# A graph kernel's edge stage in 16-bit halves, with the basis laid out four times and read by blocks of 16 lanes

## The reference

```python
p1 = tanh(h @ pp_W1 + pp_b1) @ pp_W2 + pp_b2
inter = concat(p1[src], p1[dst]) @ pi_W1 + pi_b1
inter = (inter @ pi_W2 + pi_b2) @ pi_W3
i1 = einsum('ecb,eb->ec', inter.reshape(E, 64, 8), edge_attr_8)
i1 = tanh(i1 @ ii_W1 + ii_b1) @ ii_W2 + ii_b2
x = x + segment_sum(i1, dst)
```

## Time and profile before

| | |
|---|---|
| median of 3 runs | 8050.49 us (8045.1 to 8051.35) |
| the profiled execution | 8058.17 us, of which the span is 8056.5 |
| PE, matmuls | 7250.3 us busy (90% of the span), 44520 instructions |
| PE, weight loads | 4945.0 us (61%) |
| DVE | 3022.3 us (38%) |
| ACT | 2022.9 us (25%) |
| POOL | 1563.6 us (19%) |
| DMA queue of SP (q1) | 1816.94 MB, 74.5% of the 16 DMA engines' span |

### The profile page before, as it was taken

One profiled execution on the slowest core, in us unless ns is written; L12 is line 12 of the kernel. 1 busy time (PEld: TensorE's weight loads), 2 busy tenths in 40 slices (PEclk: granted clock), 3 DMA queues, 4 the chain that ended last, 5 costly groups with the idle time before them and its releaser, 6 DMA issues. The chain is left out here.

```text
span 8056.5 us, 132776 instructions
## 1 busy us (share of the span) xinstructions
PE 7250.3 (90%) x44520; PEld 4945.0 (61%) x44520; DVE 3022.3 (38%) x4630; ACT 2022.9 (25%) x3278; POOL 1563.6 (19%) x1655
## 2 busy tenths in 40 slices
PE   4688888888888888888779999999999999999999
PEld 2577777777777777777645555555555555555554
DVE  5566666666666666666540000011100000011000
ACT  3344444444444444444300000000000000000000
POOL 2334433443443344334200000000000000000000
PEclk9799999999999999999889999999999999999999
DMA  3688888888888888888758787877788888888776
GB/s 103 164 213 213 217 210 214 214 217 211 214 216 213 213 214 217 211 214 214 174 200 281 268 281 268 280 269 279 272 295 289 295 289 290 293 290 293 266 267 228
DMA packets 828957, 1927.15 MB, mean 239 GB/s; under 512 B 66366, under 2 KB 123134, under 8 KB 828862
## 3 DMA queue, kind: packets, MB, share of 16 engines
q1 hardware_dynamic: 775564, 1816.94, 74.5%
q0 software_dynamic: 52352, 108.63, 4.3%
q10 hardware_dynamic: 946, 0.26, 0.0%
HBM read 1752.16 MB, written 173.46 MB: 239 GB/s over the span
## 5 line engine op out<-in xcount | busy, mean ns | idle before, releaser
L1199 PE MATMUL ps_a<-ring,table 128*128 128x448 fp8e4 x19208 | 3656.3, 353 | 42.8 <-DVE table L105 42.8
L1199 PEld LDWEIGHTS ps_a<-ring,table 128*128 128x128 f16 x19208 | 1881.8, 98 | 1793.4 <-DVE table L105 44.4
L593 ACT CAST unit<-ps_c 128x490 fp8e4<-128x490 f32 (+1 forms) x2548 | 1641.0, 662 | 1994.7 <-PE ps_c L734 1976.0
L560 POOL DMA_INDIRECT gathered<-u_source,plan x1576 | 1486.8, 943 | 2326.9 <-PE ps_u L756 1773.9
L734 PE MATMUL ps_c<-cell_hot,lane_hot 128*128 128x490 f16 x2548 | 889.2, 370 | 490.5 <-DVE cell_hot L643 490.5
L643 DVE TENSOR_SCALAR cell_hot<-iota_n,cell 128x490 f16<-128x490 f16 x2548 | 728.3, 343 | 378.4 <-PE ps_c L734 378.3
L1023 ACT COPY agg<-ps_a 128x448 f32<-128x448 f32 x196 | 104.3, 532 | 2930.3 <-PE ps_a L1199 2930.3
L773 PEld LDWEIGHTS ps_m<-M_sb,z 128*128 128x128 f32 x6272 | 810.2, 192 | 34.5 <-issue 0.3
L773 PEld LDWEIGHTS ps_m<-M_sb,x_sb 128*128 128x128 f32 x6272 | 810.0, 192 | 13.1
L997 POOL COPY hst<-h 128x896 f32 x28 | 26.4, 943 | 3925.8 <-PE ps_t L1211 2463.0
L773 PE MATMUL ps_m<-M_sb,x_sb 128*128 128x64 f32 x6272 | 784.7, 268 | 0.0
(11 more groups left out here) (185 smaller groups left out, 3302.1 us busy)
## 6 DMA issues: line engine op xcount, KB each, us to landing
ring<-counts SPq DMA_DIRECT2D x392, 1848.0 KB, 7.1
ring<-counts SPq DMA_DIRECT2D x196, 1792.0 KB, 7.0
basis<-in_basisT SPq DMA_DIRECT2D x198, 1024.0 KB
x_sb<-in_basisT SPq DMA_DIRECT2D x198, 1024.0 KB
counts<-unit SPq DMA_DIRECT2D x196, 784.0 KB
dst_all<-in_dst_seq SPq DMA_DIRECT2D x198, 512.0 KB
gathered<-u_source,plan POOLq DMA_INDIRECT x1576
window<-u_target SPq DMA_DIRECT2D x198, 64.0 KB
```

The source lines that it names most:

```text
L560: pool.indirect_dma_start(gathered[q][:, i, :], None, Us, bass.IndirectOffsetOnAxis(ap=T["plan"][:, at:at + 1], axis=0)).then_inc(S[f"rows ...
L593: nc.scalar.copy(unit[q][:, :, BD * i:BD * i + n], got[:, :, 0:n], saturate=False).then_inc(S["emptied"], 1)
L1199: last = mm(ps_a[:, b, 0:BC].rearrange("p (u c) -> p u c", u=BU), table[n % 2][:, k, :], cells, start=(k == 0), stop=(k == TILES - 1))
```

## The change

- `u_source` and `u_target` hold each number as two 16-bit halves, the second scaled by `LO` (2048). In the preparation ACT's copies make the first half, and DVE, in `lower(g)`, subtracts it from PSUM and scales the rest; the store waits for `low`, PE for `tb_lo`. DVE subtracts from all targets the first one of their half group, once, and SP keeps the result in `dst_local`.
- A half group of 512 edges has its own window of 64 targets (128 rows of halves), so there are two windows, two values of `base_of`, two sums and two additions a group. Window, `from_node` and `gathered` are 16-bit; `to_node` (not in the cut below) is taken against 64 targets. The join does one pass for the window and eight for `gathered`, against `id_hi` and `id_lo`.
- The bias is a product (`bias_ones` x `bias_rows`) that opens `ps_m`; DVE's addition goes, and ACT takes tanh from `ps_m` into `msg`.
- 13 buffers `cell_hot`; lanes and cells of group g + 1 are built while group g is counted. PE's and DVE's orders are new.
- `basisT` has four copies, and a basis load is eight DMAs of 16 lanes, two for each copy. They stand behind the targets and windows.

```diff
-RING = 7
...
-W = P
...
+W = 64
...
+HT = ET // 2
+COPIES = 4
...
+EH = EG // 2
...
+    Us = nc.dram_tensor("u_source", (NP, 4 * D), F16, kind="Internal").ap()
+    Ud = nc.dram_tensor("u_target", (NP + W, 4 * D), F16, kind="Internal").ap()
+    dst_local = nc.dram_tensor("dst_local", (EP + 2 * EG,), F16, kind="Internal").ap()
...
-                sp.wait_ge(S["tb_ev"], 4 * g + 4)
...
+                sp.wait_ge(S["low"], 4 * g + 4)
...
+            dve.wait_ge(S["targets"], 16)
+            nc.vector.tensor_tensor(local, targets, targets[:, :, 0].unsqueeze(2).to_broadcast([DP, 4, EH]), ALU.subtract).then_inc(S["local"], 1)
...
+            def lower(g):
+                for b in range(4):
+                    n = cols[b] // P
+                    ks = slice(4 * b, 4 * b + n)
+                    v = psB[:, b, 0:cols[b]].rearrange("p (k h d) -> p k h d", h=2, d=D)
+                    dve.wait_ge(S["tb_ev"], 4 * g + b + 1)
+                    nc.vector.tensor_tensor(rest[:, ks, :, :], v, uv[:, ks, :, 0, 0, :], ALU.subtract).then_inc(S["tb_lo"], 1)
+                    dve.wait_ge(S["tb_lo"], 4 * g + b + 1)
+                    twice = [P, n, 2, D]
+                    ch(nc.vector.tensor_scalar(uv[:, ks, 0, 1, :, :], rest[:, ks, 0, :].unsqueeze(2).to_broadcast(twice), LO, None, ALU.mult))
+                    nc.vector.tensor_scalar(uv[:, ks, 1, 1, :, :], rest[:, ks, 1, :].unsqueeze(2).to_broadcast(twice), LO, None, ALU.mult).then_inc(S["low"], 1)
...
+                if g:
+                    lower(g - 1)
+            lower(GROUPS - 1)
...
+        dst_all = two(sb, "dst_all", [P, EG], F16)
+        window = two(sb, "window", [P, 2, 2 * D], F16)
+        from_node = two(sb, "from_node", [P, EG], F16)
...
+        gathered = two(sb, "gathered", [P, ET, 2, 2 * D], F16)
...
+        cell_hot = [sb(f"cell_hot{i}", [P, TILES * BD], F16) for i in range(UB)]
...
-                rows = basisT[h:NB:2, bass.ds(g * EG, EG)]
-                rows = bass.AP(tensor=rows.tensor, offset=rows.offset, ap=[[0, D]] + [list(a) for a in rows.ap])
-                eng.dma_start(to[h * D:(h + 1) * D, :, :], rows).then_inc(signal, 16)
...
-        base_of = lambda eng, g: eng.value_load(dst_seq[bass.ds((g + 1) * EG, 1)].unsqueeze(0), min_val=0, max_val=NP - 1)
+                for i in range(COPIES):
+                    rows = basisT[i * NB + h:(i + 1) * NB:2, bass.ds(g * EG, EG)]
+                    rows = bass.AP(tensor=rows.tensor, offset=rows.offset, ap=[[0, D // COPIES]] + [list(a) for a in rows.ap])
+                    at = h * D + i * (D // COPIES)
+                    eng.dma_start(to[at:at + D // COPIES, :, :], rows).then_inc(signal, 16)
+        base_of = lambda eng, g, h: eng.value_load(dst_seq[bass.ds((g + 1) * EG + EH * h, 1)].unsqueeze(0), min_val=0, max_val=N_NODES)
...
-                    base = base_of(sp, g)
+                    bases = [base_of(sp, g, h) for h in range(2)]
                     sp.wait_ge(S["z_done"], 4 * t + 2 * q)
+                    sp.sem_inc(S["passed"], 1)
+                    sp.dma_start(dst_all[q][:, :], G["dst_local"][bass.ds(g * EG, EG)].unsqueeze(0).to_broadcast([P, EG])).then_inc(S[f"placed{q}"], 16)
+                    for h in range(2):
+                        sp.dma_start(window[q][:, h, :], Ud.rearrange("n (s d) -> (n s) d", s=2)[bass.ds(bases[h] * 2, 2 * W), :]).then_inc(S[f"placed{q}"], 16)
                     load_basis(sp, g, basis[q], S[f"loaded{q}"])
-                    sp.dma_start(dst_all[q][:, :], dst_seq[bass.ds((g + 1) * EG, EG)].unsqueeze(0).to_broadcast([P, EG])).then_inc(S[f"loaded{q}"], 16)
-                    sp.dma_start(window[q][:, :], Ud[bass.ds(base, W), :]).then_inc(S[f"loaded{q}"], 16)
...
+                        empty(t, q, range(0, UB - 1))
+                        act.wait_ge(S["m_done"], 2 + 4 * t + 2 * q + 2)
+                        nc.scalar.activation(msg[q][:, :, 0:D], ps_m[q][:, :, :], ACT.Tanh).then_inc(S[f"tanh{q}"], 1)
+                        empty(t, q, [UB - 1])
...
+                    nc.vector.tensor_scalar(from_node[q][:, :], dst_all[q][:, :], T["row_node"][:, :], T["row_scale"][:, :], ALU.is_equal, ALU.mult).then_inc(S[f"from{q}"], 1)
...
+                        dve.wait_ge(S["counted"], multiplied(g - 1, i))
+                        nc.vector.tensor_scalar(cell_hot[i][:, :], T["iota_n"][:, :], T["cell"][:, bass.ds(g * UB + i, 1)], None, ALU.is_equal).then_inc(S["cells"], 1)
...
                     for h in range(2):
+                        base = base_of(dve, g - 1, h)
+                        dve.wait_ge(S["summed"], g + 1)
+                        dve.wait_ge(S["added"], 2 * g + h)
+                        there = aggT[:, bass.ds(base, W)]
+                        nc.vector.tensor_tensor(there, there, ps_w[0:D + 1, h, :], ALU.add).then_inc(S["added"], 1)
...
+                        place_lanes(*following)
                         place_to(t, q)
-                        place_cells(t, q, range(0, 11))
-                        for h in multiply(*following):
-                            if h == 0:
-                                dve.wait_ge(S["m_done"], 4 * t + 2 * q + 4)
-                                nc.vector.tensor_tensor(msg[q][:, :, 0:D], ps_m[q][:, :, :], T["iib1"][:, :].unsqueeze(1).to_broadcast([P, ET, D]), ALU.add).then_inc(S[f"m_bias{q}"], 1)
                         place_from(t + 1, q)
-                        place_cells(t, q, range(11, UB))
-                        place_lanes(*following)
+                        place_cells(*following, range(0, 4))
+                        multiply(*following, 0)
                         add(g)
+                        place_cells(*following, range(4, 8))
+                        multiply(*following, 1)
+                        place_cells(*following, range(8, UB))
...
+                        last = mm(ps_w[0:D + 1, i // HT, :], msg[q][:, i, :], to_node[q][:, i, :], start=(i % HT == 0), stop=(i % HT == HT - 1))
...
+                def join(t, q, h):
+                    if h == 0:
+                        pe.wait_ge(S[f"from{q}"], t + 1)
+                        pe.wait_ge(S[f"rows{q}"], 16 * ET * (t + 1))
+                    pe.wait_ge(S["z_done"], 4 * t + 2 * q + h + 1)
+                    pe.sem_inc(S["passed"], 1)
+                    mm(ps_u[h][:, :], window[q][:, h, :], from_node[q][:, 512 * h:512 * h + 512], start=True, stop=False)
+                    for i in range(HT):
+                        mm(ps_u[h][:, i * P:(i + 1) * P], gathered[q][:, HT * h + i, 0, :], T["id_hi"][:, :], start=False, stop=False)
+                        last = mm(ps_u[h][:, i * P:(i + 1) * P], gathered[q][:, HT * h + i, 1, :], T["id_lo"][:, :], start=False, stop=(i == HT - 1))
+                    last.then_inc(S[f"u{q}"], 1)
...
+                        following = (t, 1) if q == 0 else (t + 1, 0)
+                        join(*following, 0)
+                        count(g, q, range(0, 4))
+                        sum_group(1 - q, t + q, g)
+                        join(*following, 1)
+                        pe.wait_ge(S[f"tanh{q}"], t)
+                        pe.sem_inc(S["passed"], 1)
+                        mm(ps_m[q][:, :, :].rearrange("p t d -> p (t d)"), T["bias_ones"][:, :], T["bias_rows"][:, :, :].rearrange("p t d -> p (t d)"), start=True, stop=False)
                         for h in range(2):
                             pe.wait_ge(S["z_done"], 4 * t + 2 * q + h + 3)
                             pe.sem_inc(S["passed"], 1)
+                            for i in range(HT):
                                 for k in range(4):
+                                    last = mm(ps_m[q][:, HT * h + i, :], z[h][:, k, i * P:(i + 1) * P], T["M"][:, k, :], start=False, stop=(h == 1 and i == HT - 1 and k == 3))
+                                if i == HT - 1:
                                     last.then_inc(S["m_done"], 1)
+                                count(g, q, [4 + HT * h + i])
+                        count(g, q, [UB - 1])
...
+        "basisT": np.tile(np.concatenate([edge_attr_8, np.zeros((pad + 2 * EG, NB), np.float32)]).T, (COPIES, 1)),
```

More of the change, by code:

```diff
@@ L447, in edges @@
         z = [sb("z", [P, 4, 512], F32), spare[:, 4 * EG:4 * EG + 2048].rearrange("p (b e) -> p b e", b=4)]
-        dst_all = two(sb, "dst_all", [P, EG], I32)
-        window = two(sb, "window", [P, 2 * D], F32)
-        from_node = two(sb, "from_node", [P, EG], F32)
+        dst_all = two(sb, "dst_all", [P, EG], F16)
+        window = two(sb, "window", [P, 2, 2 * D], F16)
+        from_node = two(sb, "from_node", [P, EG], F16)
         to_node = two(sb, "to_node", [P, ET, W], F32)
-        gathered = two(sb, "gathered", [P, ET, 2 * D], F32)
+        gathered = two(sb, "gathered", [P, ET, 2, 2 * D], F16)
         msg = two(sb, "msg", [P, ET, D + 1], F32)
         lane_hot = two(sb, "lane_hot", [P, UB, P], F16)
-        cell_hot = [sb(f"cell_hot{i}", [P, TILES * BD], F16) for i in range(RING)]
```

(32 more changed lines are left out.)

192 lines of the change are left out of this document (99 added, 93 removed).

## The result

The changed kernel takes 8946.48 us (median of 4, 8941.07 to 8980.59), the kernel before 8050.92 beside it: a ratio of 1.1122, 95% interval 1.1094 to 1.1151. Slower by 11%, where 8730 us was forecast, and inside the range.

The account below looks back on a forecast made before the run. The edge stage's ring PE to DVE to PE was taken to bound the kernel, DMA engines close behind. Profiled 8058 us + 631 (edge stage) + 50 (preparation) = 8739, median 8 lower: 8730 us; range 7650 to 9450.

Parts of the forecast that it names:

- The basis' pace: Basis loads, edge stage: pace follows lanes written, not readers of one row; 16-lane loads take 15 us, for 10.3 before.
- Between two and three: Basis load: number of 16-lane blocks in flight at once; two would take 20.5 us, three 13.7; 15 us taken.
- B: Time of the DMA engines for one group's basis load, eight loads of 16 lanes: 15 us forecast, 10.3 before.
- the far end: Basis load, rival of full lockstep: two blocks in flight or fewer, 20.5 us, kernel 9400 us; chance 0.17 with worse.
- Period = B + 7.0: Edge stage, ACT's wait for the counts' store behind the next load: basis time plus 7.0 us, 22.0 us a group.
- the 4.2 that I took at 407 GB/s: DMA engines, per group: counts 2.0, gathers 1.3 and the rest 0.9 us, all besides the basis.
- The preparation: Stage before the edge stage: DVE's lower halves and the subtraction of targets add 50 us, between 20 and 80.
- The loops: Edge stage, per group without the store's wait: PE 14.3 us, DVE 13.7, SP 14.5.
- the bare read: DVE's second base read from DRAM, before the second addition, with nothing to cover it: 2.3 us with register work.
- pace as with 64 lanes: Basis load, rival: four blocks in flight, 10.3 us, period 17.3, kernel 7810 us, faster than before; chance 0.22.
- fit into: TensorE, edge stage: idle 8 us a group; the half clock after idling (2.05 us for 1.10) costs no extra time.
- full pace: Basis load, rival: readers of a row were the brake, copies bring it near 5 us, kernel 7270 us; chance 0.12.

Follow-up runs that it names:

- the last kernel: Changed kernel with 128-lane basis loads from a table holding rows eight times, windows then store then basis, base reads moved: 7528.35 us, ratio 0.9358 to the kernel before.

## Why the prediction was right, and where it was off

- **The basis' pace, right.** "Between two and three" blocks in flight gave B = 15 us; 504 ns x 512 / 16 = 16.1. That the lanes written decide, not the readers, was read from the fast landing of `dst_all`, and three runs show it: the same 16 lanes spread out (218 GB/s), one source for all (no change), one copy and 64 lanes (202 GB/s). In the Trainium skill, "SBUF — State Buffer", section "Door 1: The DMA port swizzle", lanes 0 to 15 reach 4 ports, and lanes 0, 4, ... 60 all 8 that lanes 0 to 63 reach. The pace of the spread lanes agrees. Its 104 GB/s for 16 lanes was the far end, and 130 GB/s was measured. How many blocks were in flight no trace shows; between two and three was a guess that came out.
- **Period = B + 7.0, near, with a term too small beside it.** With B = 16.1 it gives 23.1; 22.97 was measured. But the DMA engines alone are at 0.97 x 22.97 = 22.3 us, so what is not basis takes up to 6.2 us and not the 4.2 that I took at 407 GB/s (a share reads up to 1.08 in a full stretch, so 6.2 is the most). Both bounds lie within some two microseconds, and the runs don't tell which one ends last: with the store first the period stayed 3400 / 148 = 22.97 us, but on a chip where TensorE stood still. So the slow basis is shown as the cause of the loss, and the store's wait as what sets the period is argued.
- **The size.** A group lost 4.2 us for 3.2, 191 of the 216 us missed; the term is B, 1.1 us too small. The preparation took 58 us where 50 stood.
- **The loops, right at full clock.** 14.6 us for 14.3. Half a join takes 0.82 us (from 2026.84 to 2027.66 in the timeline), 0.6 to 1.0 forecast; cells no longer hold PE; the bare read is 2.36 us, 2.3 forecast.
- **The rival "pace as with 64 lanes", wrong in its price.** With that pace the kernel takes 8193 us and not 7810, and the sign turns: it is not faster than before. The step that failed is the period of B + 7.0 = 17.3 us: the wait for the store fell in every second group, 22.1 us beside 14.6, so that the groups at full clock alone take 18.8 us in the mean, and the 18 at half clock make it 19.1. I had let the half clock "fit into" idle time. In the changed kernel it does (32 of 146 groups, no longer than the others), but not where the period is shorter: 22.1 us for 18.7 with the lanes spread, for 19.2 with the store first. Why the wait comes out longer than my sum at this pace was not tried.
- **The rival "full pace", not reached.** Copies don't bring it. Nor does a 128-lane load bring it in full.

## What to carry to other kernels

Before splitting a load, ask which lanes each piece writes, and over how many DMA engines its outermost dimension spreads: the row with the GB/s beside the share tells slow packets (full share, 130 GB/s) from idle engines (share 0.13) at once. Copies of a source are worth trying only once a load from one row to all lanes has been seen to be slow. And a store that a later group waits for does not go simply ahead of a load: with it there, the small loads that head a chain waited in its place. The fastest version has the small loads first, then the store, then the bulk, though that order was tried only together with two other edits.

## What was unexpected

- A DMA whose source has 2 as its outermost dimension used two of 16 engines: 52 GB/s at a share of 0.13. With 16 there, the same bytes moved 248 GB/s.
- In the last kernel, at a DMA share of 0.92, DVE's base read under `z` (2.29 us) still left 2.5 us bare; the pointer's read alone took up to 4.96 us there, where 1.42 was the most before.
- On two chips TensorE stood still some 5 us in most groups with no releaser in the trace, and the kernel before took 9311 and 9506 us; there the changed stage was faster than it in all five runs of four versions (0.951 to 0.963), and on the other chips slower in every version but the last (1.019 and over).
- The same idle time of TensorE did not cost the same: behind 8.59 us the next products with `M` ran at full clock, behind 3.68 us in another version at half, for the whole group. A wait of TensorE is to be priced from groups counted at either clock, not from one stretch of the timeline.
